# Second layer's expert up products from split fp32r operands, with the experts' weights split on GpSimd at the end of the first layer's mixture

## The reference

```python
x_flat = x.reshape(N, Dd)
logits = x_flat @ gate_w.T + gate_b
probs = jax.nn.softmax(logits * ROUTE_SCALE, axis=-1)
topk_vals, topk_idx = jax.lax.top_k(probs, TOPK)
dense_gate = jnp.zeros((N, E), probs.dtype).at[jnp.arange(N)[:, None], topk_idx].set(topk_vals)
h = jax.nn.relu(jnp.einsum('nd,edh->neh', x_flat, w1) + b1)
y = jnp.einsum('neh,eho->neo', h, w2) + b2
out_flat = jnp.einsum('ne,neo->no', dense_gate, y)
```

## Time and profile before

| | |
|---|---|
| median of 3 runs | 631.2 us (624.67, 631.20 and 637.21) |
| the profiled execution | 631.67 us, its span 630.0 us |
| PE busy | 563.2 us (89%) |
| DVE busy | 507.2 us (81%) |
| POOL busy | 377.2 us (60%) |
| ACT busy | 282.2 us (45%) |
| mean granted PE clock | 0.95 of full |
| DMA | 10.87 MB, 17 GB/s over the span |

### The profile page before, as it was taken

One profiled execution on the slowest core, in us unless ns is written; L12 is line 12 of the kernel. 1 busy time (PEld: TensorE's weight loads), 2 busy tenths in 40 slices (PEclk: granted clock), 3 DMA queues, 4 the chain that ended last, 5 costly groups with the idle time before them and its releaser, 6 DMA issues.

```text
span 630.0 us, 9276 instructions
## 1 busy us (share of the span) xinstructions
PE 563.2 (89%) x2934; PEld 405.8 (64%) x2934; DVE 507.2 (81%) x922; ACT 282.2 (45%) x640; POOL 377.2 (60%) x347
## 2 busy tenths in 40 slices
PE   4949999999999995889999999999999999997854
PEld 3735666666666664767767667667677676675724
DVE  7584565664765764599999999999999999999775
ACT  3612242242252244154654655645645546555332
POOL 6930010030030033339999998998999999989754
PEclk9987999999999998689999999999999999999677
DMA  8300000000000000000100000010000100000002
GB/s 255 116 2 0 2 0 2 0 1 0 2 0 2 2 0 0 1 1 2 34 0 17 17 8 25 0 33 0 17 17 0 33 0 17 17 1 0 2 0 68
DMA packets 12185, 10.87 MB, mean 17 GB/s; under 512 B 1784, under 2 KB 10624, under 8 KB 11776
## 3 DMA queue, kind: packets, MB, share of 16 engines
q1 hardware_dynamic: 12160, 10.55, 5.4%
HBM read 9.50 MB, written 1.05 MB: 17 GB/s over the span
## 4 chain that ended last, share of the span: by engine, by line
DVE 38%; PE 36%; issue 17%; ACT 5%; POOL 2%; DMA 0%; DVEq 0%; ACTq 0%; POOLq 0%
PE bank L524 34%; DVE bank L1369 10%; DVE shared L1357 9%; DVE shared L1363 7%; ACT shared L1043 3%; PE bank L527 2%; DVE shared L1392 2%; DVE shared L1377 1%; DVE ssum L1387 1%; DVE smax L1373 1%; POOL shared L469 1%; ACT shared L1041 1%; DVE z_ms L1383 1%; DVE shared L1404 1%; DVE ln_stats L1126 1%
## 5 line engine op out<-in xcount | busy, mean ns | idle before, releaser
L524 PE MATMUL bank<-xnT,w 128*128 128x512 f32 x256 | 121.1, 608 | 5.6 <-ACT shared L1055 5.6
L524 PE MATMUL bank<-w,shared 128*128 128x128 f32 x1024 | 125.1, 275 | 0.0
L524 PEld LDWEIGHTS bank<-w,shared 128*128 128x128 f32 x1024 | 119.9, 193 | 0.0
L469 POOL TENSOR_TENSOR shared<-shared 128x1024 f32<-128x1024 f32 x36 | 85.3, 2368 | 25.9 <-DVE shared L1392 25.8
L524 PE MATMUL bank<-shared 128*128 128x512 f32 (+3 forms) x280 | 89.3, 444 | 0.0
L1230 DVE TENSOR_TENSOR shared<-shared,bank 128x512 f32<-128x512 f32 x64 | 44.0, 687 | 55.9 <-PE bank L524 49.5
L935 ACT ACTIVATE shared<-bank 128x512 f32<-128x512 f32 x68 | 40.5, 598 | 97.6 <-PE bank L524 93.4
L1369 DVE TENSOR_REDUCE bank<-shared 128x64 f32<-128x2048 f32 x36 | 82.6, 2295 | 1.2
L524 PEld LDWEIGHTS bank<-xnT,w 128*128 128x128 f32 x256 | 43.9, 192 | 59.6 <-issue 35.5
L1055 ACT ACTIVATE shared<-bank,b_now 128x512 f32<-128x512 f32 x128 | 80.5, 679 | 1.4 <-ACT b_now L1073 1.2
L444 POOL TENSOR_TENSOR shared<-shared,xT 128x512 f32<-128x512 f32 x36 | 60.1, 1670 | 17.7 <-ACT shared L1025 17.7
(11 more groups left out here) (179 smaller groups left out, 915.4 us busy)
## 6 DMA issues: line engine op xcount, KB each, us to landing
w<-in_w SPq DMA_DIRECT2D x32, 64.0 KB, 1.8
w<-in_w SPq DMA_DIRECT2D x8, 256.0 KB, 2.7
shared<-in_wd SPq DMA_DIRECT2D x1, 1088.0 KB, 12.5
x<-in_x SPq DMA_DIRECT2D x4, 256.0 KB, 3.5
shared<-in_wg SPq DMA_DIRECT2D x1, 1024.0 KB, 8.2
shared<-in_wu SPq DMA_DIRECT2D x1, 1024.0 KB, 10.2
out<-x SPq DMA_DIRECT2D x4, 256.0 KB, 2.3
shared<-in_attn_w SPq DMA_DIRECT2D x1, 384.0 KB, 3.7
```

The costliest lines, as they stand in the source:

```text
L469: g.tensor_tensor(mix2[:, b % 2].rearrange("p j l m d -> p (j l) (m d)"), mix[:, b % 2, :, :, 0:2].rearrange("p j l m d -> p (j l) (m d)") ...
L524: return nc.tensor.matmul(out, lhsT, rhs, start=start, stop=stop)
```

## The change

The up products of the second layer's experts are computed like those of the first layer's mixture: as three fp32r matmuls of split operands each, instead of one fp32 matmul. For this:

- The buffer `w1` is gone. All eight experts' up weights (2 MB) are loaded at once into `shared`, over `wg` and `wu`, after these have been split.
- GpSimd splits them, expert by expert, into the places of `wgu_hi` and `wgu_lo` that the mixture's last batch has used (`split_expert`). In its program these 16 instructions stand behind the last batch's `attention_tokens` and ahead of clearing `ecmp` and `acc`.
- ACT writes `xnT_hi` of each batch behind `xnT`, in `channels_out`. GpSimd takes the lo parts (`token_rest1`), one at a time.
- ACT waits for all eight experts' splits before its first `state_in`, since what that writes lies over the raw weights.
- PE's loop over the scan's levels is written out, because the experts' places must be constants.

```diff
+        w1 = shared[:, 6 * P:6 * P + E1 * HC * P].rearrange("p (e u m h) -> p e u m h", e=E1, u=HC // 2, m=2)
...
-            for c in range(HC):
-                sp.dma_start(w1[:, c], w1_d[0, :, c]).then_inc(s(f"ld_w1_{c}"), 16)
             sp.dma_start(w2[:], w2_d[:, 0]).then_inc(s("ld_w2"), 16)
+            sp.wait_ge(s("w_lo_done"), 4)
+            sp.dma_start(w1, w1_d.rearrange("e p (u m) h -> p e u m h", m=2)).then_inc(s("ld_w1"), 16)
             with sp.Fori(0, E1 - 1) as e:
-                for c in range(HC):
-
-                    sp.wait_ge(s("ffn_up"), e * (B * HC) + (B - 1) * HC + c + 1)
-                    sp.dma_start(w1[:, c], w1_d[bass.ds(e + 1, 1), :, c].rearrange("e p h -> (e p) h")).then_inc(s(f"ld_w1_{c}"), 16)
...
+            def token_rest1(b):
+                pool.wait_ge(s("x1hi_cp"), b + 1)
+                part = slice(b * N, (b + 1) * N)
+                g.tensor_tensor(xnT_lo[:, part], xnT[:, part], xnT_hi[:, part], ALU.subtract).then_inc(s("x1lo_done"), 1)
+
+            def split_expert(e):
+
+                if e > 0:
+                    pool.wait_ge(s("u_mm"), item((B - 1) * PAIRS + 2 * e) + 1)
+                units = slice(2 * e, 2 * e + 2)
+                raw = w1[:, e].rearrange("p u m h -> p m u h")
+                g.tensor_copy(wgu_hi[:, :, units], raw).then_inc(s("w1_hi_done"), 1)
+                pool.wait_ge(s("w1_hi_done"), e + 1)
+                g.tensor_tensor(wgu_lo[:, :, units], raw, wgu_hi[:, :, units], ALU.subtract).then_inc(s("w1_lo_done"), 1)
+
             for b in range(B):
                 state_product(b)
+                if b > 1:
+                    token_rest1(b - 2)
                 if b > 0:
                     add_to_x(b - 1)
                     normalise1(b - 1)
                 attention_tokens(b)
+            token_rest1(B - 2)
+            pool.wait_ge(s("ld_w1"), 16)
+            pool.wait_ge(s("u_mm"), item((B - 1) * PAIRS) + 1)
+            for e in range(E1):
+                split_expert(e)
 
             pool.wait_ge(s("x1_done"), B)
...
+            token_rest1(B - 1)
             sum_inputs(0, 0)
...
             def expert_up(e, blk, c):
 
-                if blk == 0:
-                    pe.wait_ge(s(f"ld_w1_{c}"), e * 16 + 16)
+                if c == 0:
+                    pe.wait_ge(s("x1lo_done"), blk + 1)
+                    pe.wait_ge(s("w1_lo_done"), e + 1)
                 if c == HC - 1:
 
                     pe.wait_ge(s("ffn_relu"), (e * B + blk) * HC + 1)
-                mm(bank[UP[c]][:], w1[:, c], xnT[:, blk * N:(blk + 1) * N]).then_inc(s("ffn_up"), 1)
+                u, m = 2 * e + c // 2, c % 2
+                tokens = slice(blk * N, (blk + 1) * N)
+                mm(bank[UP[c]][:], wgu_hi[:, m, u], xnT_lo[:, tokens], True, False)
+                mm(bank[UP[c]][:], wgu_hi[:, m, u], xnT_hi[:, tokens], False, False)
+                mm(bank[UP[c]][:], wgu_lo[:, m, u], xnT_hi[:, tokens], False, True).then_inc(s("ffn_up"), 1)
...
-            with pe.Fori(0, LEVELS - 2) as lev:
+            for lev in range(LEVELS - 2):
                 level(lev)
...
                 a.copy(xnT[:, b * N:(b + 1) * N], bank[k][:]).then_inc(s("x1T_cp"), 1)
+                act.wait_ge(s("x1T_cp"), b + 1)
+                a.copy(xnT_hi[:, b * N:(b + 1) * N], xnT[:, b * N:(b + 1) * N]).then_inc(s("x1hi_cp"), 1)
...
             act.wait_ge(s("x1_done"), B)
+            act.wait_ge(s("w1_lo_done"), E1)
             state_in(0, 0, 0)
```

More of the change, by code:

```diff
@@ L115, in build @@
         gate1_w = sb("gate1_w", [P, E1])
-        w1 = sb("w1", [P, HC, P])
         b1 = sb("b1", [P, E1, HC])
@@ L268, in build @@
         for name in (
-            "ld_x0 ld_x1 ld_x2 ld_x3 ld_w1_0 ld_w1_1 ld_w1_2 ld_w1_3 ld_scan ld_gate0 ld_first ld_attn ld_l1 "
+            "ld_x0 ld_x1 ld_x2 ld_x3 ld_w1 ld_scan ld_gate0 ld_first ld_attn ld_l1 "
             "ld_wg ld_wu ld_wd ld_w2 st_out const sel_done masks "
             "polar_sq_done polar_sum_mm polar_sum_cp polar_r_done polar_x0 ln_stat ln_var_done ln_pow ln_norm "
-            "xnT_mm xnT_cp xnT_hi_cp xnT_lo_done w_hi_done w_lo_done logit_mm sig_done wfold wog_done wo_mm "
+            "xnT_mm xnT_cp xnT_hi_cp xnT_lo_done w_hi_done w_lo_done w1_hi_done w1_lo_done x1hi_cp x1lo_done logit_mm sig_done wfold wog_done wo_mm "
             "woc_done gram_mm gram_cp q_mm q_cp route0_step parts_done g0T_mm g0T_cp "
```

## The result

The median of 4 runs after is 643.04 us (639.02 to 644.24), beside 630.11 us for the 4 runs before that were made with them (624.67 to 637.21). The ratio is 1.0195, with a 95% interval of 1.0147 to 1.0243. The profiled execution took 642.88 us, its span 641.2 us, at a mean granted clock of 0.944 against 0.950. The forecast was 641.5 us in a range of 635 to 649. The interval reaches over 2%, so the forecast that the change stays within 2% is neither met nor missed. (Medians and ranges here count all runs; ratios leave out the runs more than 1.5% above the fastest of the same kernel.)

The account below looks back on a forecast made before the run. DVE was taken to bound the scan, and a chain of single instructions the mixture's end; PE's saving counted 0, the head's delay 9.9 us. From 631.67 that gave 641.6, stated as 641.5 us, range 635 to 649.

Parts of the forecast that it names:

- The bound in the scan: In the scan, DVE sets the 9.62 us slot and PE follows, waiting 0.48 us for it in each.
- The term: Up products in the scan: PE saves 0.76 us in each of 31 slots, worth 0 because DVE covers it.
- The start of the splits: End of the mixture: POOL starts splitting at 238.65, after the last batch's copy, cast and 1.27 us token rest.
- The splits: Into the head: eight experts on POOL at 2.0 us each, 16.0 us; with DVE in the way done at 255.1.
- the meeting of DVE: During the splits, DVE's addition to x slows POOL once, adding 0.46 us; bounds 0 and 3.6 us.
- The roots and the multiplication: Norm in the head: ACT's copies and roots take 1.75 us; DVE's multiplication, 0.85 us alone, ends at 258.7.
- the block: In the head, POOL's memset holds DVE's multiplication until 257.8, not 256.9; without this the shift would be 9.0 us.
- The sum: Norm's multiplication in the head ends 9.9 us later, moving the profiled execution from 631.67 to 641.6 us.
- A (splitting longer): In the head, POOL meets DVE more often or reads strided weights slower: 13.4 us, so 645.1 us; chance 0.10.
- B (clock falls in each slot): In the scan, PE's longer holes cost it its clock, 0.48 us a slot, 15 us more, 656.5 us; chance 0.06.
- C (PE the bound): In the scan, PE bounds the slot through its late turning of the state: 23.6 us go, 618 us; chance 0.03.
- D (splits hidden): In the head, splits finish before ACT needs them; only clearing and casts cost some 1.5 us: 633 us; chance 0.05.

Follow-up runs that it names:

- experiment 4: Changed kernel with GpSimd's two memsets (ecmp, acc) moved behind the scan's first last product; 641.14 us, ratio 1.0223 to the kernel before.
- experiment 2: Changed kernel splitting only four experts and using their weights twice, so the result differs; 634.92 us, ratio 1.0109 to the kernel before.
- experiment 3: Changed kernel with up products back to fp32 from their own buffer and PE's loop on the chip, splits and wait kept; 639.42 us, ratio 1.0131 to before.
- experiment 1: Changed kernel with six of eight experts' splits moved ahead of the last batch's second-layer norm on GpSimd; 631.47 us, ratio 0.9998 to before.
- 3 again: Unedited repeat of the changed kernel with fp32 up products and PE's loop, splits and wait kept; 643.34 us, ratio 1.0227 to before.

## Why the prediction was right, point by point

**The bound in the scan** was read rightly. DVE sets the slot. What PE saved became holes, 0.33 + 0.65 in place of 0.48, and the slots stayed at 9.6. The size was wrong: PE saved 0.50 us a slot and not 0.76. Of it 0.42 are the up products, which take 302.52 - 298.89 - 0.33 = 3.30 us and not 2.96; the mixture's 0.23 us from one to the next doesn't hold throughout, since the first of them starts 0.32 us ahead of the second. The term was worth nothing, so the error didn't show in the time. I had expected one hole of 1.24 us in front of DVE's wait; a part lies at ACT's relu, which sooner products run into.

**The start of the splits.** I said 238.65, which is 3.20 us ahead of the mixture's last turning on PE (241.85). After, it is 244.71 - 241.50 = 3.21 us. The chain behind it (copy, cast, token rest) was right to 0.01.

**The splits.** Forecast 16.46 us with the meeting of DVE, measured 257.18 - 241.50 = 15.68. A cast takes 0.61 and not 0.70: the line drawn between 128 and 2048 elements lies too high. The 0.46 us for one meeting with DVE was right, and only one of the sixteen instructions was made longer by it. It cost DVE's addition to x more (1.67 instead of 0.69), under cover of the same wait.

**The roots and the multiplication.** The roots took 258.92 - 257.18 = 1.74 us, forecast 1.75. The clearing ended 259.81 - 257.18 = 2.63 us behind the splits, forecast 2.70, and the multiplication 260.47 - 259.81 = 0.66 us behind the clearing, forecast 0.90: a first part lay ready when the memset ended. Against a kernel without the block I had priced it at 0.9, which took the multiplication alone for 0.85 us; it takes 1.12 (experiment 4), and the block costs 0.3. The Trainium skill's page "SBUF — State Buffer", section "Who interferes with whom", says that the later one blocks until the first has finished; the trace agrees here. The 4-element operation of experiment 2 waited longer than that: past the subtraction that was running when it began, and past two memsets that began after it.

**The sum.** 0.78 for the splits, 0.07 for the clearing and 0.24 behind it are 1.1 us less than forecast: 9.9 becomes 8.8, and five executions (three of the changed kernel, two of experiment 3's) show 8.82 to 8.85 over before's 6.99. The forecast of 641.6 for the profiled execution beside a measured 642.9 is 1.1 too high there and 2.9 too low in A and B, with 0.5 less from D on. So it was right in mechanism and within 1.1 us in the size of that wait; that the whole came out within 1.5 us is luck, for 2.9 us that I hadn't forecast stood against the others.

**The rivals.** A (splitting longer) is out by 15.68; B (clock falls in each slot) by a granted 1.00 and unchanged slots; C (PE the bound) by slots of the same length; D (splits hidden) by ACT's 11.39 us. D is what experiment 1 builds.

**What stays open.** Over all runs the median is 643.2 us after (16 runs) and 631.0 before (88 runs), 12.2 apart, and C explains 8.8. The other 3.4 must lie in A, B, D and E, if C is in all runs what it is in the profiled ones. The changed kernel's three profiled executions without unread matmuls all had the long start, before's two had the short one, but the kernels of experiments 2 and 4 and "3 again" had the short one too. Whether the long start comes oftener with the changed program, and why, these profiles are too few to tell.

## What to carry to other kernels

Where all engines run in their own order, the place of added work in the program of an engine with time to spare decides its price: 16 us of splits cost 8.8 us behind the last batch's work, and nothing that could be measured with six of the eight pairs ahead of it. Before taking time off an engine, look on the timeline whether it has a hole in each round and whom it waits for there; here the saving only widened the hole. And when a change moves the time by 1 to 2%, cut both traces at the same instructions and subtract stage by stage: the stage that changed repeated to 0.03 us, while whole runs scattered by 15.

## What the runs showed of the hardware that was not expected

- In the changed kernel, run three times, the 32 logits took 6.83 us twice (granted 0.50) and 4.05 us once; over all fourteen profiled executions they took 6.83 us in eight, 3.64 to 4.05 in five and 4.87 in one. From 18 us on the start's groups of eight took 1.75 us in one execution of experiment 3's kernel, and 1.27 and 0.98 in the other. PE had done the same work ahead of it both times. For the start, the Trainium skill's page "TensorE: Matmul & The Clock Gate", section "Part 1: The HAM clock gate (the "warmup" mystery)", says that the number of matmuls at the low rate differs from run to run; the trace agrees there, and shows the same in the middle of the program. The product of the experts' bias after the scan took 6.1 to 7.2 or 4.7 to 5.1 us. In the stages that hold these three places lies most of the scatter of the profiled executions: between the shortest and the longest with the added wait (experiment 4's and the changed kernel's second, 632.8 and 642.6), A makes 4.68 us, D 3.74, E 1.91, B and C -0.53.
- In the start's stretch the granted clock reads 1.00 in both cases, though the matmuls' lengths differ by 1.75 / 0.98 = 1.8 and PE does 30 matmuls in one and 20 in the other. Before, then after:

```profile
16.00:20.00 4.00, 4.00 (x30) 4.00 (x28) 1.52 (x1) 1.34 (x3) 3.92 (x2) 1.00 1.03 363
```

```profile
16.00:20.00 4.00, 4.00 (x20) 4.00 (x20) 1.44 (x1) 1.34 (x3) 3.92 (x2) 1.00 0.96 363
```

  There the lengths tell the speed and the column doesn't.
- Filling a wait with matmuls kept the granted clock at 1.00 in the wait (11.13 of 12 us busy) and, in that kernel, didn't keep it in the narrow matmuls behind the transposes that followed (0.50). In the kernel before, treated alike, it did (1.00).
- A DVE tensor_scalar of 4 elements a partition took 0.17 us alone, 1.43 us when it began during GpSimd's last memset, and 3.12 us when it began during a subtraction with two memsets behind it. There GpSimd's next instruction went ahead of the waiting DVE one, twice. In the changed kernel it began during a subtraction with a cast behind it, and took only 0.48.
